# Cross attention of a decoder layer: the low key term of the scores over 64 rows, two query tiles at a time

## The reference

```python
q = (Q @ Wq + bq).reshape(b, len_q, H, DIM_K).transpose(0, 2, 1, 3)      # 8 x 16 heads x 512 x 64
k = (K @ Wk + bk).reshape(b, K.shape[1], H, DIM_K).transpose(0, 2, 1, 3)
v = (V @ Wv + bv).reshape(b, V.shape[1], H, DIM_V).transpose(0, 2, 1, 3)
scale = 1.0 / np.sqrt(b).astype(np.float32)
att = jnp.einsum('bhqd,bhkd->bhqk', q * scale, k)
att = jax.nn.softmax(att, axis=-1)
out = jnp.einsum('bhqk,bhkd->bhqd', att, v)
return out.transpose(0, 2, 1, 3).reshape(b, len_q, H * DIM_V) @ Wo + bo
```

## Time and profile before

| | |
|---|---|
| median of 3 runs | 2136.64 us (2121.32 to 2143.55) |
| profiled execution, first to last instruction | 2132.4 us |
| cross attention in it | about 441 to 1873 us |
| TensorE busy over the span | 2020.7 us (95%) |
| VectorE, ScalarE, GpSimd busy | 1560.0, 1148.4, 773.3 us |
| mean granted clock of TensorE | 0.980 |

### The profile page before, as it was taken

One profiled execution on the slowest core, in us unless ns is written; L12 is line 12 of the kernel. 1 busy time (PEld: TensorE's weight loads), 2 busy tenths in 40 slices (PEclk: granted clock), 3 DMA queues, 4 the chain that ended last, 5 costly groups with the idle time before them and its releaser, 6 DMA issues. The chain is left out here.

```text
span 2132.4 us, 35254 instructions
## 1 busy us (share of the span) xinstructions
PE 2020.7 (95%) x9888; PEld 1643.9 (77%) x9888; DVE 1560.0 (73%) x3162; ACT 1148.4 (54%) x2403; POOL 773.3 (36%) x910
## 2 busy tenths in 40 slices
PE   8988888789999999999999999999999999979998
PEld 6777767667888788788878878878887888767776
DVE  4777776657777777777777767777777777867886
ACT  3333333246666666666666666666666666722221
POOL 1453343213233332333323333332333323436663
PEclk9999999899999999999999999999999999989999
DMA  3766655855354352543536446263462545221121
GB/s 138 258 257 235 234 216 217 309 167 191 92 175 160 108 178 89 180 151 107 188 108 200 147 142 197 61 204 111 136 197 68 188 111 186 80 85 55 64 79 60
DMA packets 111251, 326.76 MB, mean 153 GB/s; under 512 B 9056, under 2 KB 9056, under 8 KB 107104
## 3 DMA queue, kind: packets, MB, share of 16 engines
q1 hardware_dynamic: 111072, 324.59, 46.6%
HBM read 207.12 MB, written 83.89 MB: 136 GB/s over the span
## 5 line engine op out<-in xcount | busy, mean ns | idle before, releaser
L958 POOL TENSOR_SCALAR c_prob<-c_prob,c_rden 128x512 f32<-128x512 f32 x512 | 355.6, 695 | 950.5 <-DVE c_rden L1083 950.5
L1118 DVE TENSOR_TENSOR c_pt<-c_turned,c_pt 128x512 fp32r<-128x512 f32 x512 | 353.8, 691 | 303.6 <-ACT c_pt L1033 301.4
L1033 ACT CAST c_pt<-c_turned 128x512 fp32r<-128x512 f32 x512 | 300.4, 587 | 450.8 <-PE c_turned L1254 442.1
L1267 PE MATMUL c_av<-c_pt,c_vs 128*128 128x512 f32 x1024 | 363.8, 436 | 5.7 <-DVE c_pt L1118 5.0
L1077 DVE TENSOR_REDUCE c_negmax<-c_score 128x1 f32<-128x512 f32 x512 | 348.3, 680 | 24.5 <-issue 20.4
L1006 ACT ACTIVATE c_prob<-c_score,c_negmax 128x512 f32<-128x512 f32 x512 | 353.6, 691 | 21.4 <-issue 14.2
L1243 PE MATMUL c_score<-c_ks,c_qs 128*128 128x512 f32 x1024 | 322.3, 396 | 15.9 <-issue 11.0
L1254 PEld LDWEIGHTS c_turned<-all_ident,c_prob 128*128 128x128 f32 x2048 | 256.7, 141 | 72.7 <-POOL c_prob L958 3.0
L1254 PE MATMUL c_turned<-all_ident,c_prob 128*128 128x128 f32 x2048 | 308.8, 273 | 2.0 <-POOL c_prob L958 1.9
L1243 PEld LDWEIGHTS c_score<-c_ks,c_qs 128*128 128x128 f32 x1024 | 191.0, 188 | 65.3 <-issue 15.8
L1231 PE MATMUL c_proj<-all_first_buffer,all_second_buffer 128*128 128x512 f32 x768 | 202.2, 400 | 7.0 <-SPq L876 7.0
(11 more groups left out here) (159 smaller groups left out, 2818.5 us busy)
## 6 DMA issues: line engine op xcount, KB each, us to landing
all_second_buffer<-ctxT_scratch SPq DMA_DIRECT2D x64, 512.0 KB, 7.3
all_third_buffer<-x1T_scratch SPq DMA_DIRECT2D x16, 2048.0 KB, 13.7
c_wk<-wk_scratch SPq DMA_DIRECT2D x64, 512.0 KB, 3.4
c_wq<-wq_scratch SPq DMA_DIRECT2D x64, 512.0 KB, 5.0
c_ks<-c_ks SPq DMA_DIRECT2D x128, 256.0 KB, 3.2
ctxT_scratch<-s_wsp SPq DMA_DIRECT2D x8, 2048.0 KB, 10.7
c_y<-y_steps_scratch SPq DMA_DIRECT2D x16, 1024.0 KB, 5.8
y_steps_scratch<-c_y SPq DMA_DIRECT2D x15, 1024.0 KB, 9.0
```

The lines of the kernel that those rows point to most:

```text
L958: nc.gpsimd.tensor_scalar(prob[:, n % 2, i, :], prob[:, n % 2, i, :], rden[:, n % 2, i:i + 1], 1.0, ALU.mult, ALU.mult).then_inc(p_ready, 1)
L1033: nc.scalar.copy(pt[:, t % 2, HI, :], tpsum[:, t % 2, :]).then_inc(pt_hi, 1)
L1118: nc.vector.tensor_tensor(pt[:, t % 2, LO, :], tpsum[:, t % 2, :], as_f32(pt[:, t % 2, HI, :]), ALU.subtract).then_inc(pt_lo, 1)
L1267: ins = nc.tensor.matmul(opsum[:, n % 2, :], vs[:, u, k, n, :], pt[:, k % 2, m, :], start=(k == 0 and m == HI), stop=(k == T - 1 and m == LO))
```

## The change

For two tiles of a head (even i and i + 1), issued together, the first term of each stays a matmul over 128 rows. The second term of each is a matmul over 64 rows: for the first tile on the head's own half, for the second on the other half. Its queries there are a new buffer `qd`, a copy of the HI part of the queries made by a DMA (`double_q`), two for each Q projection, issued on SyncE's queue behind the load of the next `wq`. The term LO by LO, which the 128 rows had included, goes. A pair is issued in odd steps alone, behind the projection and ahead of the transpositions, where a tile was issued in every step, ahead of the projection. The first matmul of each tile keeps the wait of that tile on `p_exp`. VectorE's `max_tile` of odd steps moves behind `recip`.

```diff
+                def double_q(g, name):
+                    ring = int(name[1]) % 2
+                    for e in range(2):
+                        own, other = sides(e)
+                        sp.wait_ge(proj_hi, split(g, name, e))
+                        sp.dma_start(as_f32(qd[other, ring, e, :]),
+                                     as_f32(qs[own, ring, e, :])).then_inc(q_doubled[e][ring], 16)
...
                         if not final:
                             sp.wait_ge(proj_mm, made(g, "Q" + name[1]))
                             load_pair(wq, wqparts, following[0] * PAIRS + following[1], wq_loaded)
+                        double_q(g, "Q" + name[1])
                         if name == "K3" and not last:
                             load_x(nb)
...
                 def body(g, u, first, last):
                     for t in range(TILES):
-                        for tile in ahead(g, t + AHEAD_S, last):
-                            max_tile(*tile)
+                        if t % 2 == 0:
+                            for tile in ahead(g, t + AHEAD_S, last):
+                                max_tile(*tile)
                         finish_slot(g, u, t, first, last)
...
                         for tile in ahead(g, t + AHEAD_P, last):
                             recip(*tile)
+                        if t % 2 == 1:
+                            for tile in ahead(g, t + AHEAD_S, last):
+                                max_tile(*tile)
...
-                def scores(g, t):
+                def score_pair(g, t):
                     n, i = divmod(t, T)
                     head, j, e = HH * g + n, n // 2, n % 2
+                    own, other = sides(e)
                     if i == 0:
                         pe.wait_ge(proj_lo, split(*pair_slot(g, "Q", j), e))
                         pe.wait_ge(k_doubled[e], 16 * (PAIRS * g + j + 1))
-                    wait(pe, p_exp, T * head + i - 1)
-                    for m in (HI, LO):
-                        ins = nc.tensor.matmul(spsum[:, i % 2, :], qs[:, j % 2, e, i * P:(i + 1) * P],
-                                               ks[:, j % 2, e, m, :], start=(m == HI), stop=(m == LO))
-                    ins.then_inc(s_mm, 1)
+                    for d in range(2):
+                        wait(pe, p_exp, T * head + i + d - 1)
+                        nc.tensor.matmul(spsum[:, d, :], qs[:, j % 2, e, (i + d) * P:(i + d + 1) * P],
+                                         ks[:, j % 2, e, HI, :], start=True, stop=False)
+                    if i == 0:
+                        pe.wait_ge(q_doubled[e][j % 2], 16 * (PAIRS // 2 * g + j // 2 + 1))
+                    for d, (q, rows) in enumerate(((qs, own), (qd, other))):
+                        nc.tensor.matmul(spsum[:, d, :], q[rows, j % 2, e, (i + d) * P:(i + d + 1) * P],
+                                         ks[rows, j % 2, e, LO, :], start=False, stop=True).then_inc(s_mm, 1)
...
                 def body(g, u, first, last):
                     for t in range(TILES):
-                        for tile in ahead(g, t + AHEAD_S, last):
-                            scores(*tile)
                         name = slot(t, first, last)
                         if name:
                             if t % 2 == 0:
                                 bank_free(g, name, first)
                             project(g, name, u, t % 2, 2)
+                        if t % 2 == 1:
+                            for tile in ahead(g, t + AHEAD_S, last):
+                                score_pair(*tile)
                         turn(g, t)
...
-    nc = bacc.Bacc("TRN2", target_bir_lowering=False, num_devices=1)
+    nc = bacc.Bacc("TRN2", target_bir_lowering=False, num_devices=1, dynamic_dma_scratch_size=1024)
```

More of the change, by code:

```diff
@@ L809, in cross_attention @@
         ks = sc.sb("ks", [P, 2, 2, 2, S], F32R)
+        qd = sc.sb("qd", [P, 2, 2, S], F32R)
         vs = sc.sb("vs", [P, 2, T, HH, 2 * DK], F32R)
@@ L831, in cross_attention @@
         k_doubled = [sc.sem(f"k_doubled{n}") for n in range(2)]
+        q_doubled = [[sc.sem(f"q_doubled{n}{r}") for r in range(2)] for n in range(2)]
         wv_loaded, c_loaded, x_loaded = held.wv_loaded, held.c_loaded, held.x_loaded
@@ L887, in _ @@
                 load_pair(wq, wqparts, 1, wq_loaded)
+                double_q(-1, "Q0+")
                 sp.wait_ge(proj_mm, made(-1, "K1+"))
@@ L892, in _ @@
                 load_pair(wq, wqparts, 2, wq_loaded)
+                double_q(-1, "Q1+")
                 def body(g, b, h, opens, closes):
@@ L935, in body @@
                             load_pair(wq, wqparts, nh * PAIRS + j, wq_loaded)
+                            double_q(g, "Q" + name[1:])
                     if opens:
@@ L1290, in _ @@
                     if name == "V2+":
[L1291 to L1294, removed]
+                        score_pair(0, 0)
+                for t in range(2, AHEAD_S, 2):
+                    score_pair(0, t)
                 groups(pe, body)
```

## The result

The changed kernel takes 2228.18 us (median of 4 runs, 2222.83 to 2229.52) against 2138.68 us of the kernel before on the same chip: a ratio of 1.0425, 95% interval 1.0393 to 1.0456. It is slower by 4.2%. The profiled execution has a span of 2225.9 us, 93.5 more than before.

The account below looks back on a forecast made before the run. TensorE was taken to set the pace by the distance of its matmul starts. Terms -59 + 41 + 71 + 1 = +54 us gave a span of 2186 and a median of 2191 us, slower by 2.5%; range 2118 to 2265.

Parts of the forecast that it names:

- rival 2: At each switch TensorE empties and loads weights late: 138 us, 2288 in all; emptying alone 82, 2232; chance 0.22 for both.
- The overlap: On TensorE, two 64-row matmuls side by side take one distance, saving 0.23 us for each of 256 pairs: 59 us.
- Going over and back: On TensorE, two switches a pair, ahead of the short matmuls and of the transpositions, at 0.08 us each: 41 us.
- My lower half: Lower part of a switch's price on TensorE, weights still loaded ahead; its middle, 0.08 us, is half of what overlaps.
- The new waits: TensorE's second tile of a pair waits for ScalarE's exponential: 54 x 0.86 and 62 x 0.40 us, together 71.
- The first group and the last: Groups with steps without projection, bound by ScalarE and VectorE already; the saving there is less and was left out.
- The copies: `double_q`'s query copies by DMA: 1 us for the few that land late, up to 5.
- TensorE waiting for the new copies: Sign in the profile after that would show the forecast wrong altogether: TensorE held by the query copies.
- the one of a lower clock: Sign that would show the forecast wrong altogether: a granted clock below 1.00 in the stage.
- a free switch: Rival 1: going over on TensorE costs nothing and the waits eat the whole saving: +13, 2150 us; chance 0.24.
- the two faster ones: Rival 3: free switch and the second tile's wait hidden, 2078 us, or half the waits, 2114; chance 0.10 together.
- The two don't run beside each other: Rival 4: the two 64-row matmuls follow each other at 0.23 us, saving nil, 2209 us; chance 0.07.

Follow-up runs that it names:

- The two kernel pairs: 64 against 128 rows: the changed kernel 2228.18 against its order over 128 rows 2198.67 us; both with ScalarE's `o_first` moved, 2185.67 against 2156.48 us.
- the one step moved: Against the changed kernel, ScalarE's `o_first` comes in step 1 of the next head behind the exponential, not step 0 ahead: 2185.67 us; over 128 rows 2156.48.
- single short matmuls: Against the kernel before, in its order and without pairs, each tile's second matmul contracts over the head's own 64 rows: 2328.57 us, ratio 1.0891.
- The best one with 64 rows: Against the changed kernel, ScalarE's `o_first` moved behind the exponential and the query copies issued ahead of the next `wq` load: 2169.58 us, ratio 1.0154.

## Why the prediction was right, and by how much each term was off

The direction and the range held: 2228 in 2118 to 2265, slower as forecast. The size was 90 us where I had 54. That is 3 us above the band of my own forecast (2165 to 2225) and next to the 2232 of rival 2 with emptying alone, so of the rivals it speaks for that one. The terms:

**The overlap, -59.** Right. The short matmuls start together, and taking the overlap away cost 56 us.

**Going over and back, 41.** This is the term that was mis-sized, with the value of 0.08 for a switch that I took between 0 and 0.27. Measured at the starts it is 0.32 - 0.23 = 0.09 on the way in (0.10 of late load comes behind it, and shows in the way back), and 0.42 - 0.23 = 0.19 plus a first transposition longer by 0.06 on the way out: 0.34 for a round trip, 87 us for 256. Twice mine. Each switch is of two parts: the next load begins 0.32 after the effective start of the last matmul, where the next full matmul would have started after 0.23, and then its own 0.10 is in the open (0.06 ahead of transpositions). My lower half supposed "with the weights still loaded ahead, as they are in all steady rows"; that was the step that failed. The row that had the price was beside it, the 0.11 of a load that comes late. The two kernel pairs give 29.5 and 29.2 us for switch and overlap together, where I had -18.

Rival 2 set the upper end of a switch, an emptied engine and a late load, at 0.27. What was seen lies between: 0.09 of the 0.16 that I took for emptying, and all of the load. The rule of the Trainium skill ("TensorEngine Tiling (Array Packing)", Key Properties: a change of the mode drains TensorE) named the right place, and its 82 us came near to the 87. That the sum with it, 2232, is 4 us from the result is luck in part: the waits in it are 19 us too large, and some 12 us of the first group and the last are missing. The trace agrees that the next load is held at each change, for 0.09 beyond the usual distance, less than the modelled rest of a matmul; whether that is a draining of the engine it doesn't show.

**The new waits, 71.** Right in cause and in place, too large in size. They came in steps 9, 17, 25 and 1, and smaller in 5, 13, 21 and 29, and in no other step of the steady groups. The long ones are 0.77 - 0.23 + 0.11 = 0.65, not 0.86, where the 0.11 is the late load behind the wait (0.43 to the short matmuls in place of 0.32). The short ones are 0.17 to 0.24, not 0.40. The view counts 68 waits, not some 110, since a short one ends before the modelled end of the matmul ahead of it. Two parts of the 0.21 by which the long ones were too large: ScalarE's chain from the first transposition to the end of the reading took 1010.31 - 1004.95 = 5.36 with a start later by 0.06, not 5.47. I had said that each step of it starts as its forerunner leaves the engine, but in the rows of before the second cast (1013.34) had waited for the transpositions of its own step, which end then; in the changed kernel it came 0.16 sooner. And TensorE's need was 0.1 later (4.87), for the longer transposition and a V projection in place of an O. There were more long waits than I counted, 62 in place of 54: the restarts of the loop didn't take away the 8 that I had left out for them. Together 62 x 0.65 + 16 x 0.24 + 46 x 0.17 = 52 us, and the experiments took 42 off with the one step moved.

**The first group and the last, left out.** I had written that the saving there is less, and put no number on it. In the traces the stage is 92.6 us longer, from its first matmul to its last. The 14 middle groups have 70.0 of it, 5.0 each, which is what the terms make for a group: 16 x (0.34 - 0.23) + 4 x 0.65 + 0.24 + 3 x 0.17 = 5.1. The start of the stage has 2.8, the first group 10.6 and the last 9.2, some 12 more than the terms. About 7 of that are waits of the second score that are longer there; what makes the rest is open, and the lower clock of the first group may have a part in it. So -59 + 87 + 52 is 80, and with these 12 it is the 92.6. This too is a term that the forecast had at nothing.

**The copies, 1, up to 5.** Right for the changed kernel by its waits (2.6 us, 3 times), so that the sign "TensorE waiting for the new copies" came in small, as did the one of a lower clock, in the first group alone. But a hidden cost of 16 to 20 us stood behind the larger one. It appears in the kernels that have the waits for the exponential removed.

The ledger over 128 rows closes: 2136.8 without copies, 2156.5 with them, 2198.7 with ScalarE's step in its old place, 2228.2 with 64 rows: 20, 42 and 30 us. The parts are those of this order of taking things away; in the changed kernel itself the copies wait mostly under the exponential's waits.

The rivals: a free switch (2150) and the two faster ones fell with the 192 us of single short matmuls. "The two don't run beside each other" fell with the starts and with 56 us.

No version here beats the kernel before. The best one with 64 rows, with both waits taken out, stays at 2169.6, 1.5% or 33 us slower. Going over and back, less the overlap, is 29.5 of that by the pairs of kernels. By the measured numbers a visit would pay from its second pair on (an estimate: 0.34 for the round trip against 0.23 for each pair), but then four score banks are needed at once, and the stage already holds four PSUM tiles of two banks each. The Trainium skill ("Trainium Kernel Development and Optimization", NeuronCore Architecture) counts 8 banks, so another tile would have to give some up. No run here shows the limit, and none tried it.

## What to carry to other kernels

Price two half-height matmuls that run side by side as a visit, not as an instruction: here a visit cost 0.34 to 0.38 us on the way in and out, and saved 0.23 for each pair in it, so one pair for a visit loses. When a reordering makes a producer's last result be needed earlier, follow that producer's queue from a common event (here the first transposition) to the need, step by step, also on an engine that is half idle; and look at each step of that chain for whether it had waited for the engine that is to become faster. After a wait is removed, read the waits again: the next one, here the copies, was already there.

## What was not expected of the hardware

- A change of the number of rows keeps the next weight load from going ahead. In steady rows it begins with the start of the matmul before; at a change 0.32 after the effective start of that matmul, and its 0.10 is then in the open. The way back to full matmuls of 512 columns costs the same, ahead of transpositions 0.04 less.
- Two 64-row matmuls on the two halves, each with its own weights, start 3 ns apart by the records and together cost one distance: on the same half they took 56 us more in all. A second such pair right behind costs 0.20 by the time of the kernel, 0.24 by the starts, and nothing for its loads.
- Idle time as the waits view counts it understates what a wait for a semaphore costs TensorE: 30.6 us in the view where the starts show 52. A long wait of 0.37 in the view is 0.65 by the starts: some 0.17 lies under the modelled end of the matmul before, and 0.11 is the late load behind it.
